# Routing the second half of an expert stage while the first half's rows are scattered

## The reference

```python
x = x + _L0_attn_a_ref(_layernorm(x, axis=-1), ...)
x = x + _L0_ffn_ref(_layernorm(x, axis=-1), L0_ffn_gate_w, L0_ffn_expert_bias, L0_ffn_w_up, L0_ffn_w_down)
x = x + _L0_attn_b_ref(_layernorm(x, axis=-1), ...)
x = x + _L0_ffn_ref(...)        # the same weights
...                             # layers 1, 2 and 3 in the same pattern
```

```python
logits = jnp.einsum('bsd,de->bse', x, Wg) + bg
expert_idx = jnp.argmax(logits, axis=-1)
h = jax.nn.gelu(jnp.einsum('bsd,edh->bseh', x, W1) + b1, approximate=False)
y = jnp.einsum('bseh,ehd->bsed', h, W2) + b2
out = jnp.take_along_axis(y, expert_idx[:, :, None, None], axis=2)[:, :, 0, :]
```

## Time and profile before

| what | us |
|---|---|
| median of 3 runs (4129.16 to 4142.8) | 4130.23 |
| profiled execution, its own time | 4136.59 |
| span of its trace | 4134.9 |
| l0fa: first statistics to last combine | 189.99 to 513.05 |
| l0fa: first scatter, first product of the first fetched rows | 233.42, 279.25 |
| l1fa: first statistics, first scatter | 1517.74, 1553.99 |

### The profile page before, as it was taken

The page is one execution under the profiler, slowest core; times in us unless marked ns, Lnnn a source line. Parts: engine busy times, 40 slices in busy tenths (PEclk is TensorE's granted clock), DMA queues, the critical chain, the costliest instruction groups (busy, mean ns, idle before and its releaser), DMA issues. The chain is left out here.

```text
span 4134.9 us, 63879 instructions
## 1 busy us (share of the span) xinstructions
PE 2843.9 (69%) x22097; PEld 1770.2 (43%) x22097; DVE 2630.5 (64%) x5756; ACT 1794.7 (43%) x3186; POOL 1712.2 (41%) x2364
## 2 busy tenths in 40 slices
PE   4839357776295477677588856688756888577846
PEld 3739312221295256566433325333334333254534
DVE  4634568884334863252378849688667888495767
ACT  2413147775232223343246644366633466443623
POOL 6744332220443303323355534255543555344743
PEclk9969669997597668888789968699977899675967
DMA  6113132220132012102122100122000221000000
GB/s 171 43 49 92 45 108 83 75 65 1 69 90 58 10 41 60 44 1 66 53 86 86 64 1 1 63 82 76 33 1 23 87 79 63 1 1 1 1 0 21
DMA packets 217152, 206.12 MB, mean 50 GB/s; under 512 B 49431, under 2 KB 194007, under 8 KB 216072
## 3 DMA queue, kind: packets, MB, share of 16 engines
q1 hardware_dynamic: 204552, 176.85, 13.3%
q0 software_dynamic: 12288, 25.19, 1.9%
HBM read 103.55 MB, written 96.47 MB: 48 GB/s over the span
## 5 line engine op out<-in xcount | busy, mean ns | idle before, releaser
L983 DVE TENSOR_REDUCE l0b_negm<-l0b_ps_s 128x2 f32<-128x1024 f32 x256 | 304.2, 1220 | 51.2 <-PE l0b_ps_s L736 50.2
L826 ACT ACTIVATE l0b_E<-l0b_ps_t 128x1024 f32<-128x1024 f32 x256 | 262.0, 1023 | 130.4 <-PE l0b_ps_t L718 130.2
L826 ACT ACTIVATE l2a_E<-l2a_ps_t 128x768 f32<-128x768 f32 (+1 forms) x192 | 169.3, 882 | 131.6 <-PE l2a_ps_t L718 130.8
L826 ACT ACTIVATE l3a_E<-l3a_ps_t 128x768 f32<-128x768 f32 (+1 forms) x192 | 169.4, 882 | 128.5 <-PE l3a_ps_t L718 127.7
L826 ACT ACTIVATE l2b_E<-l2b_ps_t 128x768 f32<-128x768 f32 (+1 forms) x192 | 169.3, 882 | 106.3 <-PE l2b_ps_t L718 105.4
L983 DVE TENSOR_REDUCE l2b_negm<-l2b_ps_s 128x2 f32<-128x256 f32 (+3 forms) x256 | 196.4, 818 | 28.4 <-PE l2b_ps_s L741 28.3
L983 DVE TENSOR_REDUCE l3a_negm<-l3a_ps_s 128x2 f32<-128x256 f32 (+3 forms) x256 | 196.3, 818 | 16.3 <-PE l3a_ps_s L741 16.2
L983 DVE TENSOR_REDUCE l2a_negm<-l2a_ps_s 128x2 f32<-128x256 f32 (+3 forms) x256 | 196.0, 817 | 15.0 <-PE l2a_ps_s L741 14.8
L903 POOL TENSOR_SCALAR_AFFINE_SELECT l2b_E<-l2b_E 128x256 f32<-128x256 f32 x256 | 100.8, 409 | 177.6 <-ACT l2b_E L826 177.5
L903 POOL TENSOR_SCALAR_AFFINE_SELECT l2a_E<-l2a_E 128x256 f32<-128x256 f32 x256 | 101.6, 409 | 168.0 <-ACT l2a_E L826 165.8
L903 POOL TENSOR_SCALAR_AFFINE_SELECT l3a_E<-l3a_E 128x256 f32<-128x256 f32 x256 | 101.5, 409 | 167.0 <-ACT l3a_E L826 165.0
(11 more groups left out here) (970 smaller groups left out, 8702.1 us busy)
## 6 DMA issues: line engine op xcount, KB each, us to landing
room_up<-l0b_stack SPq DMA_DIRECT2D x32, 192.0 KB
room_down<-l0b_stack SPq DMA_DIRECT2D x32, 192.0 KB
room_up<-l2a_stack SPq DMA_DIRECT2D x32, 192.0 KB
room_down<-l2a_stack SPq DMA_DIRECT2D x32, 192.0 KB
room_up<-l2b_stack SPq DMA_DIRECT2D x32, 192.0 KB
room_down<-l2b_stack SPq DMA_DIRECT2D x32, 192.0 KB
room_up<-l3a_stack SPq DMA_DIRECT2D x32, 192.0 KB
room_down<-l3a_stack SPq DMA_DIRECT2D x32, 192.0 KB
```

The costliest lines, as they stand in the source:

```text
L826: act.activation(probs(n % 3, c, 0)[:, 2 * p:2 * p + 2, :], ps_t[:, :, 0:width[c]], ACT.Exp, scale=scale).then_inc(probs_ready.sem, 1)
L983: e = dve.tensor_reduce(negm[:, qt, :, j], ps_s[n % 2][:, :, off:off + keys[qt]], AX.X, ALU.max, negate=True)
```

## The change

The two halves stay. Norm, turning and router products go on in the same order, but the routing is done in two passes (`route(0)`, `route(1)`), each over 16 tiles or 128 columns. The first pass starts when the products of batch 3 are done. PE makes the counts of the first pass between the router products of batches 6 and 7; ACT takes the first exponential between XNT of batch 4 and the norm of batch 6. `slots_ready` is counted twice, so that POOL may scatter the first half after the first pass. DVE then does the first half's owners, the second pass and the second half's owners. Each half has 16 K + 7 blocks, 39 or 23, in groups of 4 with a last one of 3. For K = 2 the addition of XN to X stands in the block loop, one batch after the result of each of the groups 0 to 7. For K = 1 batches 0 to 3 are combined after groups 8, 9, 10 and 11. The scratch tensors have 88 instead of 80 blocks, and so the clearing writes more. With `parts=(4, 4)`, EARLY is 8 and equals B, and the code for more than two chunks is not in use.

```diff
-def routed_experts_stage(core, name, w, bias, up, down, top2=False, b1=None, b2=None):
+def routed_experts_stage(core, name, w, bias, up, down, top2=False, b1=None, b2=None, parts=(4, 4)):
...
-    HB = HT * K + NE
...
+    BLOCKS = [n * TB * K + NE - 1 for n in parts]
+    first_block = [sum(BLOCKS[:c]) for c in range(CHUNKS + 1)]
+    LAST = first_block[-1]
+    groups = [(c, j, min(GROUP, first_block[c + 1] - j)) for c in range(CHUNKS)
+              for j in range(first_block[c], first_block[c + 1], GROUP)]
...
+    routes = ((0, 1), (1, CHUNKS))
+    EARLY = min(B, parts[0] + 4)
...
+        def paced(c, i, n):
+            return first_block[c] + i * min(n, BLOCKS[c] - 3) // n + 1
...
             pool.wait_ge(slots_ready.sem, slots_ready.upto(1))
-            scatter(0)
-            scatter(1)
-            gather(0)
-            gather(1)
+            for i, (t, k) in enumerate(moves(0)):
...
+                scatter_row(0, t, k)
+            pool.wait_ge(slots_ready.sem, slots_ready.upto(2))
+            for i, (t, k) in enumerate(moves(1)):
+                pool.wait_ge(up_ready.sem, up_ready.upto(paced(0, i, len(moves(1)))))
+                scatter_row(1, t, k)
...
+            def counts(r):
+                c0, c1 = routes[r]
+                pe.wait_ge(chosen_ready.sem, chosen_ready.upto(r + 1))
+                pe.matmul(ps_n[r][:, c0:c1, :], core.ones[:, :], spread[:, c0:c1, :], start=True, stop=True)
+                pe.matmul(ps_c[r][:, tiles(r), :], core.earlier[:, :], both[:, tiles(r), :], start=True, stop=False, skip_group_check=True)
...
             for b in range(B):
                 if b + 1 < B:
                     rows.transposes(pe, b + 1)
-                mm = logit_products(b)
...
+                logit_products(b, int(b >= parts[0]))
+                if b == EARLY - 2:
+                    counts(0)
+            counts(1)
...
                 rows.read_transposes(act, b)
+                if top2 and b == parts[0]:
+                    expert_exponentials(0)
             if top2:
...
+                expert_exponentials(1)
...
-            for b in range(B + 1):
-                if b < B:
+            for b in range(EARLY + 1):
+                if b < EARLY:
                     rows.statistics(dve, ch, b)
                 if b >= 1:
                     rows.shifts(dve, b - 1)
...
+            route(0)
...
+            owners(0)
+            route(1)
+            owners(1)
...
                 read_y(G)
+                if top2 and G < B:
+                    add_normed(G)
                 for b in combine_at(G):
                     combine(b)
```

More of the change, by code:

```diff
@@ L2634, in routed_experts_stage @@
         y = [sb(f"y{k}", [P, GROUP, D]) for k in range(2)]
-        back = [[sb(f"back{h}_{k}", [P, HT, D]) for k in range(K)] for h in range(HALVES)]
+        back = [sb(f"back{k}", [P, NT, D]) for k in range(K)]
         if top2:
@@ L2695, in _ @@
         def _(pool):
-            for b in range(B):
+            for b in range(EARLY):
                 rows.roots(pool, b)
             pool.wait_ge(cleared.sem, 16 * core.clears)
[L2700 to L2706, removed]
@@ L2708, in gather @@
-            def gather(h):
-                for k in range(2):
[L2710 to L2716, removed]
@@ new lines, in moves, with wait_stored @@
+            def moves(c):
+                return [(t, k) for t in range(lo[c], lo[c + 1]) for k in range(K)]
+            def wait_stored(c):
+                for k in range(2):
+                    pool.wait_ge(stored[k].sem, stored[k].after(len(range(k, first_group[c + 1], 2))))
+            pool.wait_ge(slots_ready.sem, slots_ready.upto(1))
+            for i, (t, k) in enumerate(moves(0)):
+                if i % 2 == 0 and i // 2 + EARLY < B:
+                    rows.roots(pool, i // 2 + EARLY)
+                scatter_row(0, t, k)
@@ new lines, in counts @@
+            def counts(r):
[3 more added lines that the diff above has]
+                pe.matmul(ps_c[r][:, tiles(r), :], core.earlier[:, :], both[:, tiles(r), :], start=True, stop=False, skip_group_check=True)
+                for c in range(c0, c1):
+                    for t in range(lo[c], lo[c + 1] - 1):
+                        later = both[:, t:t + 1, :].broadcast_to([P, lo[c + 1] - t - 1, NE])
+                        mm = pe.matmul(ps_c[r][:, t + 1:lo[c + 1], :], core.onesb[:, :], later, start=False,
+                                       stop=(c == c1 - 1 and t == lo[c + 1] - 2), skip_group_check=True)
+                mm.then_inc(counts_in_psum.sem, 1)
@@ L2750, in transposes @@
                     pe.wait_ge(xT_ready.sem, xT_ready.upto(G - 1))
-                for k in range(GROUP):
+                for k in range(groups[G][2]):
                     tr = pe.transpose(ps_t[G % 2][:, k, :], x_in[G % RING][:, k, :], core.identf[:, :])
@@ L2812, in roots @@
                 act.activation(rstd[:, :], var[:, :], ACT.Sqrt).then_inc(roots_ready.sem, 1)
-            for j in range(ALL * GROUP):
+            for j in range(LAST):
+                if b1 is not None and j in (0, first_block[1]):
+                    act.wait_ge(b1_ready.sem, b1_ready.upto(1 + (j > 0)))
                 act.wait_ge(up_ready.sem, up_ready.upto(j + 1))
@@ L2916, in _ @@
+            for b in range(EARLY, B + 1):
+                if b < B:
+                    rows.statistics(dve, ch, b)
+                if b > EARLY:
+                    rows.shifts(dve, b - 1)
+            owners(0)
+            route(1)
+            owners(1)
             if top2:
@@ L3000, in routed_experts_stage @@
     rows.end()
-    for h in range(HALVES):
-        scattered[h].end(HT * K)
-        stored[h].end(ALL // 2)
+    for c in range(CHUNKS):
+        scattered[c].end(parts[c] * TB * K)
+    for k in range(2):
+        stored[k].end(len(range(k, ALL, 2)))
     for k in range(RING):
```

353 lines of the change are left out of this document (203 added, 150 removed).

## The result

| | before | changed |
|---|---|---|
| median of 4 runs, us | 4134.9 (4129.2 to 4142.8) | 4070.0 (4059.6 to 4079.1) |
| profiled execution, its own time and span, us | 4136.6, 4134.9 | 4079.1, 4077.3 |
| mean granted clock of TensorE, share of full speed | 0.818 | 0.820 |

The changed kernel takes 0.9841 of the time of before (95% interval 0.9809 to 0.9873). It is faster by 65 us at the medians, where 50 were forecast. Ratios compare executions in the fast state alone; one of the six of experiment 7 took 8122.0 us, for a reason that nothing here shows, and is left out there.

What follows compares the result with a forecast made beforehand. Up to the first fetch, a chain of products, routing, counts, slots and scatters bounds each expert stage. Scatter, second-pass and block terms gave 14.6 (K = 2) and 10.3 us (K = 1), two of each 49.8: 4080 us, range 4064 to 4104.

Steps and rivals of the forecast that it cites:

- First scatter, K = 2: In l0fa and l0fb the first routing pass brings the first scatter 12.0 us earlier; bounds 9.6 and 13.2.
- named good bound: In the first routing pass for K = 2, if the counts halved too, the first scatter gains 13.2 us.
- First scatter, K = 1: In l1fa and l1fb the first routing pass brings the first scatter 6.5 us earlier; bounds 5.4 and 7.7.
- The second pass beside the scatters: DVE's second routing pass stretches the first half's scatters by 0.18 us each, costing 1.0 us a stage.
- Taking them out of their old place gives nothing: Removing the additions of XN to X from ahead of the loop gains nothing, as POOL was scattering then.
- Blocks: Two blocks fewer a stage in PE's loop save 3.6 us for K = 2 and 4.8 us for K = 1.
- Additions in the loop: Eight additions in each K = 2 loop, 0.69 us each, fit DVE's idle of 1.53 us and cost nothing.
- The fourth rival: In K = 2 loops each addition delays a copy as a combine does, 6.6 us each: 4186 us, chance 0.04.
- Rivals 1 and 3: Beside DVE every scatter stretches 0.54 us, 4098 us, chance 0.09; or DVE and POOL exclude each other fully, 4140, chance 0.02.
- Rival 2: The first routing pass doesn't come early, so only the blocks count, 16.8 us: 4113 us, chance 0.05.

Runs made afterwards that it cites:

- experiment 7: Three-part kernel (2, 4 and 2 batches, stages with two choices) with two of its waits taken away and earlier counts in stages with one choice: 4034.5 us.
- experiment 1: Changed kernel with the routing of both halves made in one pass after the last batch, all else as changed: 4113.1 us, 0.9943 of before.
- experiment 4: Changed kernel with the eight additions of X and XN back between gates and loop of each stage with two choices: 4070.2 us, 0.9836 of before.
- experiment 5: Changed kernel with 24 more additions, or 32 copies, on DVE between gates and loop of stages with two choices: 4076.3 and 4074.2 us, one run each.
- experiment 2: Changed kernel with 40 and 24 blocks a half in place of 39 and 23, routing in two passes: 4089.2 us, 0.9895 of before.
- experiment 8: Each combine inside the loop cut in two: with the kernel of experiment 7 3994.9 us, alone with the changed kernel 4037.9 us.
- 9: First kernel of 8, with no scatter of the second part waiting for the first part's blocks: 3990.3 us, 0.9646 of before.
- first kernel of 8: Three-part kernel of experiment 7 with each combine inside the loop cut in two: 3994.9 us, 0.9664 of before.
- experiments 3: Changed kernel with TensorE taking the counts of stages with one choice after the products of batch 4, not batch 6: 4065.3 us, 0.9828 of before.
- second kernel of experiment 8: Changed kernel, two parts, with each combine inside the loop cut in two and nothing else: 4037.9 us, 0.9762 of before.

## Why the prediction was right, and where its sizes were off

Forecast 49.8 us, stages 65.3, difference 15.5, by terms:

- **First scatter, K = 2.** 12.0 forecast, 13.2 measured twice. The chain came as worked out (choice over at 215.8 against a stage that began 2.6 us later, 213.2 on the old scale; foreseen 213.3). What was off was the counts: left at 2.47 us "since I have no row that lets them shrink", they took 1.55, the 15 narrow matmuls 1.03. That was the named good bound.
- **First scatter, K = 1.** 6.5 forecast, 7.6 twice. From counts to scatter 7.2 became 5.3, 0.9 more than foreseen, again the counts for the most part. These two terms make 4.4 of the 15.5.
- **The second pass beside the scatters.** The step that failed, in its sign. Forecast was a loss of 1.0 us a stage; gained were 1.3 and 1.6, and 0.4 and -0.3, which makes 7.0 of the 15.5. I had taken one average of 0.18 us over all eight scatters of the earlier trace rows and laid it on any DVE work. Experiments 1, 4 and 5 show that the cost hangs on what DVE does: the additions of 512 columns stretched the scatters before and had gone; 50 small instructions left 14 scatters at 0.99 us. Where K = 1 there were no such additions to go, and the second pass did cost 0.4 us a stage (experiment 1), under half of the forecast. What the four instructions of L2980 (184 columns, two operands) cost the scatter beside them is not one number there: it took 1.22 us in l1fa and 1.62 in l1fb, and nothing here says why. "Taking them out of their old place gives nothing" was wrong for the scatters by 0.8 to 1.3 us a stage.
- **Blocks.** 3.6 and 4.8 forecast; 3.4, 4.4, 7.0 and 5.0 measured, and by experiment 2 alone 3.8, 3.1, 5.0 and 5.0. l1fa's 2 us more are the clock: the first 20 us of its loop ran at 0.73 before and 0.85 after. Loops 3.0 of the 15.5; tails, which the forecast left as they were, the last 1.0.
- **Additions in the loop.** Nothing, as said (experiment 4). The fourth rival's price was real, its place was not: experiment 8 shows what a combine costs, because ACT waits there for DVE, and for an addition no engine stands still: DVE's own next wait is 0.99 us for 1.53, and the turned rows are copied as soon after the group's result as before (2.28 and 2.22 us).
- **Rivals 1 and 3** fall with the changed kernel's own scatters (0.99 us each) and with experiment 5: back-to-back wide additions cost 0.19 us a scatter, neither 0.54 nor an instruction. The rule of the Trainium skill (SBUF — State Buffer, "Who interferes with whom") names copies as what blocks GpSimd's descriptors, for the whole instruction, and infers that a two-input addition leaves them alone. Here the additions stretched every scatter by 0.19 us and the copies only some, by up to 0.25, so the measurement decides against that size and that order.
- **Rival 2** falls with experiment 1: the first pass's place alone is worth 42.8 us, the blocks 16.9, and together they are within 6 us of the stages' sum; the rest is the additions and the clock of one loop.

## What to carry to other kernels

Where a chain of small steps ends in a long train of transfers, cut the chain at the first train's own inputs; its gain is the distance between its last input and everyone's, read from the engine that feeds them. A duration next to another engine's work is a property of that work's form: look which scatter was stretched by what before laying an average on other work. And when more parts win at both ends and lose in the middle, list the waits of the middle: each here had its own cause. Three small moves took l0fa's loop from 208.0 us to 204.1, 186.1 and 181.0, and the largest of them, the cut combines, pays without the third part as well.

## What the runs showed that was not expected

- Equal loops end up to 4.7 us apart by TensorE's granted clock in their first 20 us. The loops of K = 1 with 46 blocks took 119.4 us where it was 0.84 to 0.88, 121.1 and 121.4 at 0.74 and 0.72, and 124.0 or 124.1 at 0.58 (one stage each in experiments 7, 9 and the first kernel of 8); in the 40 us after them all ran at 1.00. A loop that starts 4.5 us earlier gave back 1.7 or all of it that way (experiments 3 and 7). What decides on the clock there stays open. Columns as in the earlier trace rows; l1fa before and changed, and l1fb of experiment 7:

```profile
1579.24:1599.24 20.00, 18.25 (x106) 16.38 (x107) 3.79 (x7) 8.03 (x25) 5.83 (x6) 0.73 0.13 39
```

```profile
1543.60:1563.60 20.00, 18.25 (x121) 16.24 (x122) 4.91 (x9) 8.47 (x27) 6.00 (x7) 0.85 0.20 59
```

```profile
1783.40:1803.40 20.00, 18.26 (x86) 16.31 (x87) 3.09 (x6) 6.78 (x21) 4.69 (x5) 0.58 0.10 29
```

- A combine's 5.61 us on TensorE were ACT's: it had 4.99 us to wait for DVE's statistics, between two table loads of 1.28 us, while later blocks' Gelus stood behind. Put two blocks later, it waits 1.53 us. The changed kernel, and then the second kernel of experiment 8:

```profile
380.93 0.21 ACT L2867 ACTIVATE l0fa_rstd<-l0fa_var 128x4 f32<-128x4 f32 x1 [4.99 <-DVE l0fa_var L3049]
```

```profile
375.30 1.28 ACT L2867 ACT_TABLE_LOAD   x1
...
378.11 0.20 ACT L2867 ACTIVATE l0fa_rstd<-l0fa_var 128x4 f32<-128x4 f32 x1 [1.53 <-DVE l0fa_var L3058]
378.33 1.28 ACT L2877 ACT_TABLE_LOAD   x1
```

- Why the scatters beside the before kernel's eight additions took 1.16 and 1.50 us and then 0.96 twice in l0fa, and 1.42, 1.50 and 1.50 in l0fb, while 24 additions in a row gave an even 1.15, stays open. So does the scatter of 1.62 us in l1fb of the changed kernel, beside the four instructions of L2980:

```profile
1810.04 1.62 DVE L2980 TENSOR_TENSOR l1fb_pick<-l1fb_own,l1f_b 128x184 f32<-128x184 f32 x4
1810.89 1.62 POOL L2729 DMA_INDIRECT rows_in<-XN,l1fb_slot_u  x1 [0.30 <-issue]
```
